# A three-layer graph network on one core: where the last 128 rows of a group's gather come from

## The reference

```
x = x + gnn(layernorm(x), (src, dst), edge_type)
x = x + ffn(layernorm(x))
# gnn, L = 3 layers
xr = einsum('nd,rde->rne', x, W_rel[l]); msg = xr[edge_type, src]
x = relu(segment_sum(msg, dst) + x @ W_root[l] + bias[l])
# ffn: sign(sign(x) @ sign(w).T) * exp(logsumexp_k(log(|x|+eps) + log(|w|+eps))) + bias
```

## Time and profile before

| what | value |
| --- | --- |
| median of 3 runs | 5964.4 us |
| span of the profiled execution | 5964.9 us |
| POOL busy | 4396.5 us (74%), 4659 instructions |
| PE busy | 4310.7 us (72%) |
| DVE busy | 1844.7 us (31%) |
| ACT busy | 619.0 us (10%) |
| gathers (L403) | 4633, 947 ns each, 1316.2 us of issue time before them |
| row DMAs (L352) | 7168, 1.0 KB each |
| mean granted TensorE clock | 0.884 |
| DMA engines busy | about 3 tenths, 113 GB/s |

### The profile page before, as it was taken

How to read it: one execution, slowest core, us unless ns; L and a number is a source line. 1 busy time by engine, 2 the same in 40 slices (tenths; PEclk the granted TensorE clock), 3 DMA queues, 4 the chain that set the end, 5 groups by cost and what they waited for, 6 DMA issues and landing times.

```text
span 5964.9 us, 107654 instructions
## 1 busy us (share of the span) xinstructions
PE 4310.7 (72%) x26040; PEld 3901.4 (65%) x26041; DVE 1844.7 (31%) x3589; ACT 619.0 (10%) x848; POOL 4396.5 (74%) x4659
## 2 busy tenths in 40 slices
PE   4777777777777767777777777766776777776776
PEld 3666666666676656666666666666676666666666
DVE  5222222222222222222222222223333334333333
ACT  3001010010101000000000001000101011101111
POOL 5777777777777677777777777767777777777774
PEclk8898989898989888889999999888888888888887
DMA  6333333333333333333333333333333333333332
GB/s 196 113 111 113 112 112 112 111 114 111 113 112 112 107 111 110 111 111 111 110 111 111 111 110 112 110 106 113 114 113 115 113 113 114 114 113 114 113 113 74
DMA packets 296167, 674.77 MB, mean 113 GB/s; under 512 B 86202, under 2 KB 147387, under 8 KB 295772
## 3 DMA queue, kind: packets, MB, share of 16 engines
q0 software_dynamic: 222384, 607.55, 35.2%
q1 hardware_dynamic: 44686, 37.38, 2.1%
q10 hardware_dynamic: 28702, 26.46, 1.3%
HBM read 645.38 MB, written 25.68 MB: 112 GB/s over the span
## 4 chain that ended last, share of the span: by engine, by line
PE 27%; POOL 25%; issue 20%; SPq 15%; DMA 6%; DVEq 3%; DVE 3%; ACT 1%; ACTq 0%
POOL rows L403 25%; PE bank L421 15%; SPq L352 13%; PE bank L492 10%; DMA rows<-node_table,idx 5%; SPq L347 3%; DVE agg L1003 1%; ACT agg L708 1%; DVEq L986 1%; DVEq L989 1%; PE bank L618 1%; DVEq L1093 1%; PE bank L611 0%; DVE onehot L908 0%; PE bank L537 0%
## 5 line engine op out<-in xcount | busy, mean ns | idle before, releaser
L403 POOL DMA_INDIRECT rows<-node_table,idx x4633 | 4389.2, 947 | 1504.1 <-issue 1316.2
L421 PE MATMUL bank<-onehot,rows 128*128 128x128 f32 x18792 | 2700.1, 305 | 1422.5 <-DVE agg L1003 705.8
L421 PEld LDWEIGHTS bank<-onehot,rows 128*128 128x128 f32 x18792 | 2564.0, 218 | 1571.8 <-issue 1553.2
L1003 DVE TENSOR_TENSOR agg<-bank,agg 128x256 f32 x1566 | 663.7, 424 | 2079.8 <-PE bank L421 1575.6
L492 PE MATMUL bank<-wrel,agg 128*128 128x256 f32 x5568 | 1273.8, 388 | 44.4 <-DVE agg L1016 34.2
L492 PEld LDWEIGHTS bank<-wrel,agg 128*128 128x128 f32 x5568 | 1073.4, 195 | 200.0 <-issue 53.9
L908 DVE TENSOR_TENSOR onehot<-bank,key 128x1152 f32<-128x1152 f32 x525 | 707.0, 1347 | 0.0
L708 ACT COPY agg<-zero_col 128x2304 f32 x174 | 367.2, 2111 | 2928.9 <-PE bank L492 2928.9
L1025 DVE SCALAR_TENSOR_TENSOR acc<-bank,in_first,acc 128x256 f32 x174 | 84.2, 484 | 1777.6 <-PE bank L492 1680.9
L611 PE MATMUL bank<-wroot,nextT 128*128 128x256 f32 x392 | 146.7, 510 | 0.0
L715 ACT COPY acc<-bank 128x256 f32 (+1 forms) x98 | 36.5, 372 | 1004.7 <-PE bank L611 1004.7
(11 more groups left out here) (138 smaller groups left out, 800.1 us busy)
## 6 DMA issues: line engine op xcount, KB each, us to landing
far_rows<-node_table SPq DMA_DIRECT2D x7168, 1.0 KB
rows<-node_table,idx POOLq DMA_INDIRECT x4633
node_table<-new_x ACTq DMA_DIRECT2D x98, 128.0 KB
x_tile<-node_table SPq DMA_DIRECT2D x58, 128.0 KB, 2.2
x_in<-in_x_dram SPq DMA_DIRECT2D x8, 768.0 KB, 11.2
wrel<-in_L_gnn_W_rel_dram SPq DMA_DIRECT2D x6, 1024.0 KB, 8.2
xres<-in_x_dram ACTq DMA_DIRECT2D x48, 128.0 KB
out_dram<-res ACTq DMA_DIRECT2D x48, 128.0 KB
```

The costliest lines, as they stand in the source:

```text
L403: pool.indirect_dma_start(rows[:, s:s + D], None, tables[layer % 2], bass.IndirectOffsetOnAxis(ap=idx[:, g * TPG + k, j:j + 1], axis=0),). ...
L421: last = nc.tensor.matmul(to[:, h, :], of[:, s:s + P], hot[:, hot_k * CH + j, :], start=(j == 0), stop=(j == CH - 1))
L1003: nc.vector.tensor_tensor(window, seg[k % 3].rearrange("p h (r w) -> p h r w", r=R), window, ALU.add).then_inc(agg_added, 1)
```

## The change

- Every group but the last (57, in all three layers) has its last chunk fetched by row. POOL issues 26 gathers for each of these groups, 4518 in all, for 4633 before.
- Of the 128 rows, SP fetches 72 and ACT 56. They go to two buffers `far_rows[0]` and `far_rows[1]` in turn, each with its own semaphores.
- The source numbers are loaded from `src` as four rows of 32 for each group (`far_at`), and DVE shifts them left by 10 once, so that they are byte offsets. A row's DMA goes from a view of the table as bytes, at that offset.
- ACT issues its part for the next group inside a group, in two parts, one of 32 rows and one of 24. The first stands behind `ended` (and xT), the second behind `next_sums`. In layer 2 the feed-forward's part from magT on becomes `out_of_tile` and stands between the two.
- DVE takes the fetched rows at the start of each group; group 0 of each layer is fetched ahead of its first group.
- SP's weights of the next layer are now loaded ahead of its wait for `stored`.
- The loop over extra tiles on DVE is merged to one loop, with k from a multiplication and a division. It runs only for groups whose nodes spread over more than a tile.

```diff
-FETCHED = GROUPS // 2 - 1
-HALF = P // 2
+FETCHED = GROUPS - 1
 LOADS = 32
+QUARTERS = P // LOADS
+SP_ROWS = 72
+ACT_ROWS = P - SP_ROWS
+SP_HALF = SP_ROWS // 2
...
+    table_bytes = [t.rearrange("n d -> (n d)").bitcast(u8).unsqueeze(0) for t in tables]
...
+        def far_row(p, b):
+            return far_rows[b][p:p + 1, :].bitcast(u8)
+        def far_from(layer, at_byte):
+            return table_bytes[layer % 2][:, ds(at_byte, ROW_BYTES)]
+        def far_starts(engine, g, q, first, end):
+            _, starts = nc.values_load_multi_w_load_instructions(
+                far_at[q:q + 1, ds(g * LOADS + first, end - first)], engines=[engine], ...)
+            return starts
...
+            def fetch(layer, g, b):
+                sp.wait_ge(far_copied, g + (layer * FETCHED + 1))
+                sp.sem_inc(sp_mark, 1)
+                for q in range(QUARTERS - 1):
+                    first, end = q * LOADS, min(SP_ROWS, (q + 1) * LOADS)
+                    for p, start in zip(range(first, end), far_starts(SP, g, q, 0, end - first)):
+                        sp.dma_start(far_row(p, b), far_from(layer, start)).then_inc(far_by_sp[layer][b][p // SP_HALF], 16)
+            load_tile(0, 0)
+            sp.wait_ge(far_at_ready, 1)
+            fetch(0, 0, 0)
+            with sp.Fori(0, (TILES - 1) // 2) as i:
+                fetch(0, i * 2 + 1, 1)
+                load_tile(i * 2 + 1, i * 2 + 1)
+                fetch(0, i * 2 + 2, 0)
+                load_tile(i * 2 + 2, i * 2 + 2)
...
+            for layer in range(1, L):
+                sp.wait_ge(out_ready, layer * GROUPS)
+                load_weights(layer)
+                sp.wait_ge(stored, 16 * TILES * layer + 16)
+                fetch(layer, 0, 0)
+                with sp.Fori(0, FETCHED // 2) as i:
+                    fetch(layer, i * 2 + 1, 1)
+                    fetch(layer, i * 2 + 2, 0)
...
-                        for j in range(CH - 1 if layer and g % 2 and k == TPG - 1 else CH):
+                        for j in range(CH - 1 if k == TPG - 1 else CH):
...
+            def fetch_quarter(layer, g, b, q, first):
+                for m, start in enumerate(far_starts(SCALAR, g, q, first, LOADS)):
+                    act.dma_start(far_row(q * LOADS + first + m, b), far_from(layer, start)).then_inc(far_by_act[layer][b], 16)
+            def fetch_first(layer, g, b):
+                act.wait_ge(far_copied, g + (layer * FETCHED + 1))
...
+                fetch_quarter(layer, g, b, QUARTERS - 1, 0)
+            def fetch_second(layer, g, b):
+                fetch_quarter(layer, g, b, QUARTERS - 2, SP_ROWS % LOADS)
+            def fetch_ahead(layer, g, part):
+                with act.If(g < FETCHED - 1):
+                    ahead = nc.s_assert_within(g + 1, 1, FETCHED - 1, ...)
+                    with act.If(g % 2 > 0):
+                        part(layer, ahead, 0)
+                    with act.Else():
+                        part(layer, ahead, 1)
...
             def group(layer, g, late=None):
...
-                if late and layer < L - 1:
+                fetch_ahead(layer, g, fetch_first)
+                if late:
                     with act.If(g < late[0]):
-                        next_sums(layer, late[1])
+                        if layer < L - 1:
+                            next_sums(layer, late[1])
+                        else:
+                            out_of_tile(late[1])
+                fetch_ahead(layer, g, fetch_second)
                 act.wait_ge(out_ready, gg + 1)
...
+            dve.wait_ge(far_at_loaded, 16)
+            nc.vector.tensor_single_scalar(far_at[:, :], far_at[:, :], ROW_SHIFT, ALU.arith_shift_left).then_inc(far_at_ready, 1)
...
-            def take_fetched(layer, g):
+            def take_fetched(layer, g, b):
                 for h in range(2):
-                    dve.wait_ge(far_fetched[layer - 1][h], g * (8 * HALF) + 8 * HALF)
+                    dve.wait_ge(far_by_sp[layer][b][h], g * (8 * SP_HALF) + (2 - b) * 8 * SP_HALF)
+                dve.wait_ge(far_by_act[layer][b], g * (8 * ACT_ROWS) + (2 - b) * 8 * ACT_ROWS)
                 held(g)
                 s = (TPG * CH - 1) * D
-                nc.vector.tensor_copy(rows[:, s:s + D], far_rows[:, :]).then_inc(far_copied, 2)
+                nc.vector.tensor_copy(rows[:, s:s + D], far_rows[b][:, :]).then_inc(far_copied, 1)
```

More of the change, by code:

```diff
@@ L32 @@
 XCHUNKS = 8
-FETCHED = GROUPS // 2 - 1
-HALF = P // 2
+FETCHED = GROUPS - 1
 LOADS = 32
+QUARTERS = P // LOADS
+SP_ROWS = 72
+ACT_ROWS = P - SP_ROWS
+SP_HALF = SP_ROWS // 2
+ROW_BYTES = D * 4
+ROW_SHIFT = 10
+NINTH, NINTH_SHIFT = 57, 9
+assert all((j * NINTH) >> NINTH_SHIFT == j // TPG for j in range(TILES * TPG))
 LN_EPS = 1e-5
@@ L99, in gnn_ffn @@
         code_x = sb("code_x", [P, CH], fp32)
-        far_rows = sb("far_rows", [P, D], fp32)
+        far_rows = [sb(f"far_rows{i}", [P, D], fp32) for i in range(2)]
         rows_x = sb("rows_x", [P, CH * D], fp32)
@@ L271, in gnn_ffn @@
         REST = FULL_TRIPLES - FULL_BLOCKS * P
+        def far_row(p, b):
[4 more added lines that the diff above has]
+            _, starts = nc.values_load_multi_w_load_instructions(
+                far_at[q:q + 1, ds(g * LOADS + first, end - first)], engines=[engine], min_val=0, max_val=(N - 1) * ROW_BYTES,
+                skip_runtime_bounds_check_because="sources are nodes")
+            return starts
         block = ctx.enter_context(nc.Block())
@@ new lines, in _ @@
+            sp.wait_ge(far_at_ready, 1)
[5 more added lines that the diff above has]
+                load_tile(i * 2 + 2, i * 2 + 2)
+            with sp.Fori((TILES - 1) // 2, FETCHED // 2) as i:
+                fetch(0, i * 2 + 1, 1)
+                load_tile(i * 2 + 1, TILES - 1)
+                fetch(0, i * 2 + 2, 0)
+                load_tile(i * 2 + 2, TILES - 1)
@@ L692, in _ @@
             act.wait_ge(ends_loaded, 16)
+            act.wait_ge(far_at_ready, 1)
+            def fetch_quarter(layer, g, b, q, first):
[3 more added lines that the diff above has]
+                act.wait_ge(far_copied, g + (layer * FETCHED + 1))
+                if not isinstance(g, int):
+                    act.sem_inc(act_mark, 1)
+                fetch_quarter(layer, g, b, QUARTERS - 1, 0)
[3 more added lines that the diff above has]
+                with act.If(g < FETCHED - 1):
+                    ahead = nc.s_assert_within(g + 1, 1, FETCHED - 1, skip_runtime_bounds_check_because="the branch is taken in front of the last fetched group")
+                    with act.If(g % 2 > 0):
+                        part(layer, ahead, 0)
+                    with act.Else():
+                        part(layer, ahead, 1)
+                    act.sem_inc(act_mark, 1)
             def group(layer, g, late=None):
@@ L767, in _ @@
                     act.dma_start(xres[:, :], x[0:P, :]).then_inc(x_res_loaded, 16)
+                if layer:
+                    act.wait_ge(stored, 16 * TILES * layer + 16)
+                fetch_first(layer, 0, 0)
+                fetch_second(layer, 0, 0)
                 first = act.value_load(end_row[0:1, 1:2], min_val=1, max_val=GROUPS)
@@ L782, in _ @@
                             next_sums(layer, t - 1)
+                        else:
+                            out_of_tile(t - 1)
                     if layer < L - 1:
@@ L788, in _ @@
                     next_sums(layer, TILES - 1)
+                else:
+                    out_of_tile(TILES - 1, last=True)
             act.wait_ge(x_res_loaded, 16 * TILES)
```

113 lines of the change are left out of this document (44 added, 69 removed).

## The result

The changed kernel takes 6507.8 us (median of 4 runs, 6504.2 to 6509.7), the kernel before 5968.9 (median of 4 beside them): ratio 1.0903, 95% interval 1.0887 to 1.0918. That is slower, as forecast, but 428 us above the forecast of 6080 and above the range's end of 6320. The profiled execution's span is 6504.8 us.

What follows compares the result with a forecast made beforehand. POOL's gather issue was taken to bound layers 0 and 1, a 34.1 us chain layer 2's tile-ending groups. On a span of 5964.9, -71 - 36 + 17 + 198 + 8 = +116 gave 6080 us, range 5900 to 6320.

Steps and rivals of the forecast that it cites:

- Rival 1: ACT between sign and magT in layer 2: rows at 0.26 us, deciding from about 0.29 down; 5910 us; chance 22%.
- Rival 2: ACT's jumps over the new odd/even bodies: one more a group costs 2.4 us; total 6310 us; chance 13%.
- Rival 3: Row fetches: the byte form doesn't cheapen a row, 0.42 us; total about 6740 us; chance 7%.
- 31.1 under 32.5: Layers 0 and 1: 31.1 us from DVE's start to DVE's start, under the 32.5 us of POOL's 26 gathers.
- ACT in layers 0 and 1: ACT's fetch parts of 13.3 and 10.1 us and other work fit a group: 31.3 us under 32.5.
- ACT in layer 2: First fetch part between sign and magT, second behind out's store: tile-ending groups take 39.0 us, layer 2 +198 us.
- a ring over ACT's fetch and DVE's start of a group: Layers 0 and 1: fetch, landing, DVE's copy, nextT, next fetch; 31.1 us a group.
- From DVE's copy to nextT: Layers 0 and 1: the copy of far rows was taken to be 5.4 us ahead of nextT.
- Landing: Time for the fetched rows to land: 1.5 us taken, 2.2 us for a 128 KB tile as upper bound.
- the path by the second part: Layer 2, tile-ending group: ACT's store of out, second part, landing, then DVE's next start; 39.0 us.
- that by magT and L512: Layer 2, tile-ending group: magT reaches PE 4.1 us later and all behind it moves; 34.1 becomes 38.2 us.
- One sign named beforehand: The forecast would be wrong if layer 0's group periods passed 33.8 us.

Runs made afterwards that it cites:

- Experiment 3: The changed kernel with dummy matmuls on TensorE in its idle time, read by nothing: 6347.3 us, ratio 1.0629 to the kernel before.
- Experiment 5: The changed kernel with 88 rows on SP's queue and 40 on ACT's: 6697.9 us, ratio 1.1218 to the kernel before.
- experiment 4: The changed kernel with far rows named by row number again, not by byte offset: 7046.6 us, ratio 1.1809 to the kernel before.

## Why the prediction was wrong

What held. Gathers: 4518. The row: without FUSED_REGOPS, with the MOVE, 0.32 for 0.34. ACT's fetch: 24.0 for 23.8 us with the copy between. SP: 26.6 us for the rows and loads from first to last, and between groups 6.2 and 3.3 in turn, 31.4 for 30.8 a group in layer 0 (the terms written down add up to 30.7); not the bound. The start of layer 0: DVE's first copy at 116.3 us, forecast 115. Layer 2's order, with the first part between sign and magT. Rival 1 was wrong in its point of decision: rows came at 0.32 to 0.325, and even the 0.29 that it asks for would, by the measured ring of layer 2, leave it at 42.2 - 32 x 0.035 = 41.1 us, or 40.2 if all 56 rows count. Rival 2, ACT's branches, fell: the rows start 2.28 us behind nextT's end (median, layer 1), of which the load of 32 values takes 1.98, so that 0.3 us are left for the branches and jumps there. Rival 3 fell by the rows of L362.

What failed is the step "31.1 under 32.5" of the part "ACT in layers 0 and 1", in two terms of its sum, and the same error in "ACT in layer 2". The mechanism, a ring over ACT's fetch and DVE's start of a group, was told rightly; layer 1's ring measures 24.0 for 24.2, 2.9 for 1.5 and 8.1 for 5.4, together 35.0 us for 31.1:

1. **From DVE's copy to nextT: 5.4 taken, 7.8 to 8.4 measured.** The 5.4 came from a group in which PE had been idle for 1.8 us and the granted clock was 1.00. In the changed kernel PE has been idle for 10, and comes back at the lower clock (0.50; 24 matmuls 4.71 us for 2.92); the rest is DVE's stretch from the copy to its first add (2.2 for 1.6 us), which has two loads of 0.84 us in it (L1053, L1056); the first starts with the copy, where in the group of the earlier trace rows it started 0.5 us ahead. Experiment 3 gives 1.7 to 2.2 us of it back.
2. **Landing: 1.5 taken, 2.7 in the group shown, medians of 2.9 (layer 1) and 4.0 (layer 0).** They are counted like the forecast's, from the end of the last row's DMA instruction on; from its start they are 3.3 (over all groups of layer 1) and 4.2. No row had two queues issuing at once, and the upper bound named, the 2.2 us of a tile of 128 KB, was none. In the 6 us ahead of ACT's last row SP issues 17 rows in layer 0 and 8 in layer 1 (medians), where it is done 2.6 us before ACT, and none in layer 2, where the copy follows the last row's start by 1.8 us.
3. **Layer 2: 39.0 taken, 42.2 measured.** The forecast moved "all behind" magT by 4.1 us, with the 6.6 us from the products to the store of out as they were. They take 8.3: the products start at the lower clock (0.50) in 33 of 49 tiles, before in one. Experiment 3 brings them back to 6.7 and gives 1.8 of the 3.2 us back, so PE's clock is more than half of it. Experiment 5 showed besides that my account of which path ends last was too simple: the path by the second part (39.0) and that by magT and L512 (38.2) were told as 0.8 us apart, and both turned out some 3 us longer.

The sum follows. Layer 0: a group of 36.0 us in place of 32.5, 57 x 3.5 = 200 of the 210 us. Layer 1: 33.5 in place of 32.5, 57 of the 59. Layer 2: 48 x 3.2 = 154, beside the 155; groups without a tile end add 9 x 2 (28.6 us for 26.6), and its first groups, shorter than the median, take as much back. I had written that nothing is late "if the sum stays under 32.5", found it 1.2 and 1.4 us under, and let it be over only by dear jumps or dear rows (rivals 2 and 3): a ring that close to the bound was worth a rival of its own. With layer 2's 3.2 us it would have been the 6500 that came. One sign named beforehand did come true, layer 0's periods passed 33.8.

POOL's gathers alone do not make the landing late. In layers 0 and 1 of experiment 5 they move as much as in the changed kernel while the last row is under way (about 100 GB/s in the 4 us ahead of the copy), and with SP alone issuing, its last row is copied 1.8 us after its start. What stays open: whether two queues would be late without the gathers, for no run took them away. In experiment 4, with rows spaced wider and both queues issuing, it is 2.3 us in layers 0 and 1.

## What to carry to other kernels

Rows that are issued one by one from a compute engine's queue take their time in that engine's order (here 24.0 us of ACT's for 56 rows, with one copy between): write down the ring (issue, landing, the reader's start, back to the issuer), and where it is within a tenth of the bound (here 31.1 under 32.5 us), expect that it may be the bound. The wait added ahead of a group left TensorE idle for 10.1 us in the group shown, and the 24 matmuls that followed took 4.71 us, most of them at a granted clock of 0.50, for 2.92 at 1.00; price such work at rows behind an idle stretch as long, not at those of a busy one. Put the wait in front of the one reader (here the ninth triple), and leave out the stage that has no slack (here layer 2): both together turned a ratio of 1.09 into 0.987.

## What the runs showed of the hardware

- A row of 1 KB by a computed address costs 0.319 us on SP and 0.325 on ACT by byte offset, 0.408 and 0.380 by row number; the DMA instruction on ACT takes 235 ns in the first form and 222 in the second (stretches shown above), on SP 225 in both.
- The last row is copied 1.8 us after its start (median) with one queue at work (layer 2; layers 0 and 1 of experiment 5), 4.2 with the other queue issuing up to the end (layer 0) and 3.3 where it ends 2.6 us earlier (layer 1), both at 0.32 us a row, but 2.3 with both at 0.38 and 0.41.
- Behind DVE's copy TensorE's first matmuls ran at a granted clock of 0.50 in 103 of 108 groups of layers 0 and 1, after idle time of 10.9 and 10.4 us (medians); with dummy matmuls in that time in 18. They raised the mean granted clock from 0.83 to 0.957, and the kernel ran 160 us shorter with half as many matmul records more (39256 for 26040).
